# A Macaron block on one core: FFN 2 in two token groups, most of its rows routed during attention

## The chip, the core and the metric

The kernel is one program on one core of a Trainium2 chip. The metric is device time in microseconds (us), of three runs. The engines named here are TensorE (PE, with its weight loads as PEld), VectorE (DVE), ScalarE (ACT), GpSimd (POOL) and SyncE (SP), which issues most of the DMAs; SP's own rows of the profile are called SPq.

## The reference

The input is `x`, 4 batches of 512 tokens of 256 numbers, all in float32. With T = 2048 tokens, E = 16 experts, F = 128 and top-2 routing, the block is

```
x = x + 0.5 * ffn(layernorm(x))
x = x + attention(layernorm(x))          # 3 heads, each as wide as the model; mean of heads, fc, bias
x = x + 0.5 * ffn(layernorm(x))          # the same weights again

ffn(x): scores   = sigmoid(x @ gate_w)
        selected = top_2(scores + expert_bias);  w = their scores / (their sum + 1e-20)
        shared   = silu(x @ sg) * (x @ su) @ sd
        routed   = sum over the 2 selected e of  w_e * (silu(x @ G_e) * (x @ U_e) @ D_e)
attention(x): per head  Q, K, V = x Wq', x Wk', x Wv';  softmax(Q K' / 16) V
              then the mean over the heads, @ fc_w' + fc_b
```

## The kernel before, in words

**Exact products.** Each float32 operand is split into a high and a low part, and a product is three matmuls (`three_pass`: hi·hi, hi·lo, lo·hi). So every operand goes through two copies: ACT writes the high part from PSUM, DVE subtracts it and writes the low part. Transposes are matmuls with an identity.

**Stages.** (1) Norm and routing of all 16 token tiles (a tile is 128 tokens). (2) FFN 1. (3) Attention: 48 units (batch, head, block of 128 keys), 12 to a batch. (4) Norm and routing for FFN 2. (5) FFN 2. (6) Gather of the expert outputs, sum, shared expert, store.

**An FFN** works on sorted rows. Each of the 4096 (token, expert) pairs gets a slot; an expert's slots start at a multiple of 128. So `SLOT_TILES = 4096/128 + 15 = 47` tiles hold them in every case, each with the weights of one expert. `ffn(r, between)` walks steps `s`, the same loop on each engine: in step `s`, tile `s` is transposed (PE), split into `xt_ring` (ACT, DVE), tile `s-1` goes through gate and up (6 matmuls), its silu and product are formed, tile `s-3`'s hidden is transposed and split, tile `s-4` goes through down (3 matmuls), is copied to `y_buf` by ACT and stored to `y_dram` by SP. That is 47 + 4 steps. `between(s)` runs at the end of a step on each engine. PE reads the weight offsets of four tiles at a time from SBUF into registers (`pick_weights`). POOL gathers each tile's rows from `xn_dram` with an indirect DMA (`load`), up to 4 ahead.

**Routing** for r = 1 stands in the gap between attention and FFN 2: `front_turn`, `front_hi`, `front_lo` turn and split the normed rows of all batches, `front_router` gives the logits of batch 3, `choose` picks the two experts (tiles 0 to 11 during attention, 12 to 15 in the gap), `rank_tokens` counts tokens of each expert by matmuls with a triangle of ones, `slots` turns that into slots, `pick_tiles`, `pick_lanes`, `scale_tokens` and `index_tokens` invert the slots into a gather list, `experts` gives the weight offsets, `routing_weights` the two weights. Matmuls without use (`stay_busy`) stand between.

**Order.** Every engine runs its own program in the order written. In attention the extra work is cut into pieces by generators that all engines advance in step: `side_pieces(u, ...)` takes one piece in the middle of a unit (on POOL before the unit's `e_sp` subtraction, on DVE between the row maximum and the reciprocal), `side_pieces_late` takes one at the unit's end (batches 1 and 2: every unit; batch 3: from the unit `PER_BATCH // 2` on). `previous_front(b)` holds the norm, the float32 router and the routing of batch b-1. PE mixes the values of unit w about two units after its scores; `mix` of the last two units stands behind the loop.

**End.** `gather_pair(1, t)` on POOL reads the two expert outputs of each token from `y_dram` (32 indirect DMAs, 16 semaphores, a wait for landing at each eighth); `combine` on DVE adds them times their weights; the shared expert runs on PE, ACT and DVE (`shared_gu`, `shared_silu`, `shared_mul`, `shared_hi`, `shared_lo`, `shared_y`, `shared_sink`); SP stores each tile. All of it waits for the last tile of FFN 2.

## Time and profile before

| | |
|---|---|
| median of 3 runs | 578.79 us (578.08 to 579.34) |
| the profiled execution | 576.65 us |
| its span, first to last instruction | 575.4 us |
| mean granted TensorE clock | 0.939 of full |
| busy: PE, PEld | 465.3 us (81%), 408.9 us (71%) |
| busy: DVE, ACT, POOL | 337.1 (59%), 272.6 (47%), 253.8 us (44%) |
| chain that ended last | PE 57%, DVE 16%, issue 9%, ACT 6%, DMA 5%, POOL 5% |

A row of a timeline gives start, duration, engine, line, operation, output<-inputs and count, and in brackets how long the engine had been idle and what released it. PE rows overlap by about 0.15 us, since matmuls are pipelined; the distance between starts is the better measure. Line 324 is the helper of every three-pass product, so its rows are told apart by their operands.

### The profile page before, as it was taken

Reading aid. Unit: us, or ns where it says so; the run is one execution under the profiler, and the core shown is the slowest. Engines: PE = TensorE matmul, PEld = TensorE weight load, DVE = VectorE, ACT = ScalarE, POOL = GpSimd, SP = SyncE. Lnnn points to the kernel's source line nnn. Section 1 sums busy time; section 2 is a strip of 40 time slices with the busy share of each in tenths; the row PEclk is TensorE's granted clock in tenths of the full one; section 3 lists DMA queues with packets and bytes.
Section 4 is the critical chain, followed back from the end, with each engine's and each line's share of the span. In section 5 each row is a group of like instructions: output and inputs, shape, how many; then the busy total and the mean of one; then the engine's idle time right before and its main releaser. Section 6 shows DMA issues by size and latency. Waiting matters only on the chain.

```text
span 575.4 us, 9851 instructions
## 1 busy us (share of the span) xinstructions
PE 465.3 (81%) x3029; PEld 408.9 (71%) x3029; DVE 337.1 (59%) x925; ACT 272.6 (47%) x740; POOL 253.8 (44%) x259
## 2 busy tenths in 40 slices
PE   1675599999867997999899988999786799997432
PEld 0344488888655996898789977999755789886321
DVE  5478665555284666377538763635766566663554
ACT  4758266666424444345344544447333666662010
POOL 5356765553152542363237321422204555534655
PEclk9977799999989999999899999999897999999776
DMA  8642356466321100020001100003011455562444
GB/s 302 238 129 92 110 183 179 149 202 147 105 61 59 47 1 0 21 65 27 1 19 56 38 2 1 9 29 111 1 36 49 136 167 161 168 140 92 128 132 133
DMA packets 37808, 53.61 MB, mean 93 GB/s; under 512 B 5568, under 2 KB 30528, under 8 KB 37760
## 3 DMA queue, kind: packets, MB, share of 16 engines
q1 hardware_dynamic: 29760, 32.25, 16.8%
q0 software_dynamic: 7584, 20.72, 14.0%
q8 instruction: 27, 0.44, 0.3%
q14 instruction: 21, 0.17, 0.1%
q10 hardware_dynamic: 416, 0.02, 0.0%
HBM read 34.37 MB, written 18.61 MB: 92 GB/s over the span
## 4 chain that ended last, share of the span: by engine, by line
PE 57%; DVE 16%; issue 9%; ACT 6%; DMA 5%; POOL 5%; another core or an unknown queue 0%; SPq 0%; ACTq 0%; POOLq 0%; DVEq 0%
PE bank L324 47%; POOL late_pair L1545 4%; PE bank L330 3%; PE bank L543 2%; DMA late_pair<-y_dram,slot_i 2%; DMA raw<-xn_dram,gather_at 2%; PE bank L489 2%; DVE x_sb L1297 1%; DVE softmax_row L1418 1%; DMA x_sb<-in_x 1%; DVE e_sp L1307 1%; PE bank L376 1%; DVE v_sp L1428 1%; ACT v_sp L991 1%; DVE pick_lane L1180 1%
## 5 line engine op out<-in xcount | busy, mean ns | idle before, releaser
L1580 POOL DMA_INDIRECT raw<-xn_dram,gather_at x94 | 90.4, 962 | 87.3 <-PE bank L330 37.2
L1621 POOL TENSOR_TENSOR e_sp<-raw,e_sp 128x512 fp32r<-128x512 f32 x48 | 62.7, 1307 | 127.8 <-ACT e_sp L988 127.6
L324 PEld LDWEIGHTS bank<-v_sp,e_sp 128*128 128x128 f32 x576 | 75.5, 193 | 3.2 <-POOL e_sp L1621 0.3
L324 PE MATMUL bank<-v_sp,e_sp 128*128 128x256 f32 x576 | 77.7, 285 | 0.0
L324 PE MATMUL bank<-g_sp,xT 128*128 128x512 f32 x288 | 75.7, 398 | 1.4 <-DVE g_sp L1323 1.4
L979 ACT ACTIVATE raw<-bank,softmax_row 128x512 f32<-128x512 f32 x48 | 33.2, 692 | 58.0 <-DVE softmax_row L1418 57.9
L324 PEld LDWEIGHTS bank<-g_sp,xT 128*128 128x128 f32 x288 | 52.1, 190 | 11.0 <-DVE g_sp L1323 1.8
L1418 DVE TENSOR_REDUCE softmax_row<-bank 128x1 f32<-128x512 f32 x48 | 32.9, 686 | 38.0 <-PE bank L324 37.7
L324 PE MATMUL bank<-w_hi,e_sp 128*128 x188 | 50.5, 292 | 0.6 <-DVE e_sp L1307 0.6
L1307 DVE TENSOR_TENSOR e_sp<-bank,e_sp 128x128 fp32r<-128x128 f32 x94 | 27.4, 291 | 39.3 <-ACT e_sp L862 33.2
L324 PE MATMUL bank<-w_hi,v_sp 128*128 128x256 f32 x64 | 20.4, 397 | 35.5 <-DVE v_sp L1084 30.0
L324 PE MATMUL bank<-b_sp,xT 128*128 128x256 f32 x288 | 43.9, 288 | 3.7 <-DVE v_sp L1428 3.5
L324 PE MATMUL bank<-w_hi,xT 128*128 x188 | 45.4, 304 | 1.6 <-DVE xT L1311 1.6
L324 PE MATMUL bank<-w_hi,xt_late 128*128 x188 | 45.4, 304 | 1.4 <-DVE xt_late L1311 1.2
L1428 DVE SCALAR_TENSOR_TENSOR v_sp<-bank,softmax_row,v_sp 128x256 fp32r<-128x256 f32 x48 | 23.2, 484 | 34.9 <-ACT v_sp L991 34.3
L1545 POOL DMA_INDIRECT late_pair<-y_dram,slot_i x32 | 30.3, 948 | 29.6 <-DMA y_dram<-stage 13.3
L330 PE MATMUL bank<-ident,raw 128*128 128x128 f32 x212 | 41.2, 276 | 2.7 <-DMA raw<-xn_dram,gather_at 2.5
L885 ACT COPY stage<-bank 128x256 f32<-128x256 f32 x94 | 35.6, 378 | 15.9 <-PE bank L324 11.2
L324 PEld LDWEIGHTS bank<-w_hi,v_sp 128*128 128x128 f32 x64 | 16.0, 289 | 38.0 <-DVE v_sp L1084 31.9
L878 ACT ACTIVATE raw<-bank 128x128 f32<-128x128 f32 x94 | 26.7, 284 | 34.1 <-PE bank L324 29.1
L324 PEld LDWEIGHTS bank<-b_sp,xT 128*128 128x128 f32 x288 | 38.1, 190 | 6.2 <-DVE v_sp L1428 5.3
L1537 POOL DMA_INDIRECT stage<-y_dram,slot_i x32 | 31.4, 980 | 22.7 <-DMA y_dram<-stage 14.9
(204 smaller groups left out, 1086.7 us busy)
## 6 DMA issues: line engine op xcount, KB each, us to landing
y_dram<-stage SPq DMA_DIRECT2D x94, 128.0 KB
xn_dram<-xn_all SPq DMA_DIRECT2D x5, 512.0 KB, 4.3
stage<-in_w_pack SPq DMA_DIRECT2D x6, 384.0 KB, 5.4
raw<-in_w_pack SPq DMA_DIRECT2D x6, 384.0 KB, 3.1
x_sb<-in_x SPq DMA_DIRECT2D x4, 512.0 KB, 7.7
out<-x_sb SPq DMA_DIRECT2D x16, 128.0 KB
stage_more<-in_w_pack SPq DMA_DIRECT2D x5, 384.0 KB, 3.4
xn_dram<-raw SPq DMA_DIRECT2D x12, 128.0 KB, 1.7
```

The lines of the kernel that those rows point to most:

```text
L324: m = pe.matmul(dst, lhs[k][l], rhs[k][r], start=(first and k == 0 and i == 0), stop=(last and k == n - 1 and i == 2), skip_group_check=True)
L330: m = pe.transpose(dst[:, k * P:(k + 1) * P], src[:, k * P:(k + 1) * P], ident[:])
L878: act.activation(h_buf[:, g % 2, :], bank[GU_BANKS[g % 2]][:, 0:F], ACT.Silu).then_inc(s_silu, 1)
L885: act.copy(y_buf[:, d % Y_BUFS, :], bank[Y_BANKS[d % 2]][:, 0:H]).then_inc(s_y_copy, 1)
L979: act.activation(e32[:, i, :], bank[S_BANKS[i]][:], ACT.Exp, bias=row_max[:, i, :], accum_out=row_sum[:, i, :]).then_inc(s_exp, 1)
L1307: dve.tensor_tensor(ht_rows[:, v % 2, 1], bank[HT_BANK][:, 0:P], ht_rows[:, v % 2, 0].bitcast(F32), ALU.subtract).then_inc(s_hT_lo, 1)
L1418: dve.tensor_reduce(row_max[:, i, :], bank[S_BANKS[i]][:], AX, ALU.max, negate=True).then_inc(s_max, 1)
L1428: dve.scalar_tensor_tensor(out=v_sp[:, i, 1, :], in0=bank[V_BANK][:, 0:H], scalar=row_inv[:, i, :], in1=v_sp[:, i, 0, :].bitcast(F32), op0 ...
L1537: pool.indirect_dma_start(pair_buf[:, n % PAIRS, :], None, y_dram, at).then_inc(s_pair[n % PAIRS], 16)
L1545: pool.indirect_dma_start(late_pair[:, n, :], None, y_dram, at).then_inc(s_late[n % LATE_SEMS], 16)
L1580: pool.indirect_dma_start(row_buf[:, n % ROWS, :], None, xn_dram, bass.IndirectOffsetOnAxis(ap=gather_at[:, n:n + 1], axis=0)).then_inc(s_ ...
L1621: pool.tensor_tensor(e_sp[:, i, 1, :], e32[:, i, :], e_sp[:, i, 0, :].bitcast(F32), ALU.subtract).then_inc(s_e_lo, 1)
```

## The change

FFN 2's tokens are cut into two groups: batches 0 to 2 (`LATE_T = 12` tiles) and batch 3. Each group has its own tiles: `12*2 + 15 = 39` and `4*2 + 15 = 23`, together 62.

The sorted rows are no longer gathered by a list. `slab_dram` holds for each expert a slab of rows for each group. A token's place is its expert's base plus its rank so far, and POOL scatters the normed row to both its places (`slab_row`, 2 indirect DMAs a tile) out of `xn_late`, which DVE writes a second time (`row_again`). This is done batch by batch in new pieces of `previous_front`: `choose` for four tiles (now from an exponential on ACT, +1, reciprocal), `rank_again` (5 small matmuls), `slab_rows`, and for batch 3's turn `tile_table`, `pack_table`, `write_table`, `pair_slots`, `routing_weights` of the first group. SP clears the 128 rows behind each expert's last one (`clear_rest`, 16 DMAs of 128 KB from `zero_rows`), once for each group, and reads each tile with a plain DMA at an offset it loads from the table four at a time (`load_row`).

The gap between attention and FFN 2 is gone: FFN 2 begins after the last mix but one. The last mix, the norm and routing of batch 3, the second clear and the turning of all rows for the shared expert are pieces of `late_front` between steps 1 and 36 of FFN 2; `reload_batch` stands at steps 3, 5 and 7. `pick_tiles`, `pick_lanes`, `scale_tokens`, `index_tokens`, `stay_busy` are not called for r = 1. Gathers of the first group's pairs begin while FFN 2 still runs (pair n after tile 44 + n), and DVE sums one a step from step 48 (`early_combine`, 18 pairs); 8 places and semaphores instead of 32 and 16.

```diff
+    LATE_T = (B - 1) * TB
+    LATE_TILES = (LATE_T * TOPK + E - 1, TB * TOPK + E - 1)
+    SPLIT_TILE = LATE_TILES[0]
+    PAIRS_FROM = 44
+    COMBINE_FROM = 48
+    EARLY_COMBINED = 9
@@ side_pieces_late
-            if b == B - 1 and u % PER_BATCH >= PER_BATCH // 2:
+            if b == B - 1 and u % PER_BATCH >= PER_BATCH // 3:
@@ PE, previous_front
                 yield from prev_front(b - 1)
+                yield
+                rank_again(b - 1)
+                yield
+                yield
                 if b == B - 1:
-                    yield from choose(b * TB)
+                    yield
+                    pack_table(False)
...
@@ PE, pieces of FFN 2's steps
+            def late_front():
+                yield
+                mix(U - 1)
...
+                front_turn(1, FRONT_PAIRS - 2)
...
+                front_turn(1, FRONT_PAIRS - 1)
...
+                front_router(1, B - 1)
+                yield
+                turn_scores(1, B - 1)
...
+                rank_again(B - 1)
...
+                pack_table(True)
...
+                for n in range(FRONT_PAIRS - BATCH_PAIRS):
+                    yield
+                    yield
+                    front_turn(1, n)
+                    yield
@@ PE, behind attention
-            for w in MIXED_LATER:
-                if w == U - 1:
-                    front_turn(1, 0)
-                    front_turn(1, 1)
+            for w in MIXED_LATER[:-1]:
                 mix(w)
...
-            ffn(1, lambda s: None)
+            late_side = late_front()
+            ffn(1, lambda s: next(late_side, None))
@@ ACT
+                front_sigmoid(1, B - 1)
+                act.wait_ge(s_inv_sum, U)
+                act.wait_ge(s_warm, 2)
+                act.activation(row_sum[:, 0], minus_half[:, 0:1], ACT.Silu).then_inc(s_warm, 1)
@@ DVE, previous_front
+                for t in range((b - 1) * TB - 2, (b - 1) * TB):
+                    if t >= 0:
+                        row_again(t)
+                    yield
                 measure(b - 1)
                 yield
                 yield from prev_front(b - 1)
+                run(choose(1, (b - 1) * TB, b * TB))
+                yield
+                slab_rows(b - 1)
+                row_again((b - 1) * TB)
+                yield
+                row_again((b - 1) * TB + 1)
+                yield
                 if b == B - 1:
-                    yield from choose(1, 0, SPLIT_AT)
+                    row_again(b * TB - 2)
+                    tile_table(False)
+                    yield
+                    row_again(b * TB - 1)
+                    yield
+                    write_table(False)
+                    yield
+                    pair_slots(False)
+                    yield
+                    routing_weights(1, 0, LATE_T)
+                    yield
@@ DVE
+            def row_again(t):
...
+                dve.wait_ge(s_slab[t % 2], 16 * TOPK * (t // 2))
+                norm_rows(xn_late[t % 2], t).then_inc(s_again, 1)
@@ POOL
+            def slab_row(t):
+                if t % TB == 0:
+                    pool.wait_ge(s_addr, t // TB + 1)
+                if t < LATE_T:
+                    pool.wait_ge(s_again, t + 1)
+                src, done = (xn_late[t % 2], s_slab[t % 2]) if t < LATE_T else (xn_all[:, t, :], s_slab_late)
+                for k in range(TOPK):
+                    pool.indirect_dma_start(slab_dram, bass.IndirectOffsetOnAxis(
+                        ap=addr_i[:, k, t:t + 1].bitcast(U32), axis=0), src, None).then_inc(done, 16)
@@ POOL, gather_pair
-                        if n and n % BURST == 0:
...
+                        if PAIRS_FROM + n < TILES[1]:
+                            pool.wait_ge(s_xt, BASE[1] + PAIRS_FROM + n)
@@ POOL, previous_front(3), behind the last slab_row
+                    pool.wait_ge(s_comb, NT * TOPK)
+                    pool.memset(zero_rows, 0.0).then_inc(s_zeros, 1)
@@ SP
+            def load_row(n, rows):
...
+                if i == 0:
+                    sp.wait_ge(s_zero, 16 * E * (1 + late))
+                    sp.wait_ge(s_experts, 2 + late)
+                if i % PER_LOAD == 0:
...
+                if n >= ROWS:
+                    sp.wait_ge(s_xt, BASE[1] + n - ROWS + 1)
+                sp.dma_start(row_buf[1][:, n % ROWS, :], slab_dram[bass.ds(rows["at"][i % PER_LOAD], P), :])
+            def clear_rest(late):
+                sp.wait_ge(s_zero_at, 1 + late)
+                sp.wait_ge(s_zeros, 1)
+                for e in range(E):
+                    sp.dma_start(slab_dram[bass.ds(at[e % PER_LOAD], P), :], zero_rows).then_inc(s_zero, 16)
+            def late_front(s):
+                if s in (3, 5, 7):
+                    reload_batch((s - 3) // 2)
+                if s == 16:
+                    clear_rest(True)
```

## Rows read from the trace of the kernel before

**Rows 1.** Windows: length; PE, PEld, DVE, ACT, POOL busy (count); clock; DMA share; GB/s

```profile
235.00:293.00 58.00, 55.02 (x350) 49.64 (x349) 37.64 (x88) 26.68 (x62) 25.53 (x22) 0.97 0.09 28
351.00:406.60 55.60, 55.60 (x374) 51.22 (x373) 27.07 (x98) 30.29 (x65) 16.77 (x14) 1.00 0.12 39
406.60:440.70 34.10, 25.06 (x150) 19.18 (x148) 25.10 (x70) 12.55 (x30) 4.26 (x5) 0.80 0.06 20
440.70:522.20 81.50, 73.05 (x565) 67.15 (x564) 45.35 (x141) 51.26 (x188) 42.40 (x45) 1.00 0.54 149
522.20:575.40 53.20, 22.24 (x96) 18.53 (x96) 25.23 (x48) 4.41 (x8) 30.34 (x32) 0.76 0.40 122
```

**Rows 2.** Timeline of PE in the gap: two front turns, the router

```profile
406.61 1.04 PE L376 MATMUL bank<-ident,xn_all 128*128 128x128 f32 x8
...
421.16 1.57 PE L324 MATMUL bank<-xT,gate_sp 128*16 128x512 f32 x6 [0.70 <-DVE xT L1072]
```

**Rows 3.** Timeline of PE in FFN 1: a fold (L489), then the next tile

```profile
85.87 1.89 PE L489 MATMUL bank<-route 128*128 128x256 f32 x8
...
87.71 0.38 PE L330 MATMUL bank<-ident,raw 128*128 128x128 f32 x2
```

**Rows 4.** Timeline of DVE in the gap: statistics, the start and end of one choice, a scan

```profile
410.93 1.40 DVE L1031 BATCH_NORM_STATS2 stats<-x_sb 128x6 f32<-128x256 f32 x4
...
424.09 0.23 DVE L1114 TENSOR_TENSOR route<-bank,bias_sb 128x64 f32<-128x64 f32 x1 [2.98 <-PE bank L398]
...
425.90 0.23 DVE L1140 TENSOR_TENSOR choice<-route 128x64 f16<-128x64 f32 x1
...
426.74 0.20 DVE L1151 TENSOR_TENSOR_SCAN ends<-unround,rounded 128x17 f32<-128x17 f32 x1
```

**Rows 5.** Timeline of ACT: one table load

```profile
420.40 1.28 ACT L789 ACT_TABLE_LOAD   x1
```

**Rows 6.** Timelines of POOL, DVE, then PE, in the last units of batch 1

```profile
284.92 1.33 POOL L1621 TENSOR_TENSOR e_sp<-raw,e_sp 128x512 fp32r<-128x512 f32 x1 [4.90 <-ACT e_sp L988]
...
285.13 1.39 DVE L1297 TENSOR_TENSOR x_sb<-x_sb,route 128x256 f32<-128x256 f32 x1
...
287.60 0.68 DVE L1418 TENSOR_REDUCE softmax_row<-bank 128x1 f32<-128x512 f32 x1
289.39 0.42 DVE L1287 TENSOR_TENSOR xT<-bank,xT 128x256 fp32r<-128x256 f32 x1 [1.11 <-ACT xT L846]
...
289.87 3.02 PE L324 MATMUL bank<-xT,a_sp 128*128 128x512 f32 x12 [1.16 <-DVE xT L1287]
```

**Rows 7.** Timelines of POOL, then PE, in the first units of batch 2 of attention

```profile
302.95 0.96 POOL L1537 DMA_INDIRECT stage<-y_dram,slot_i  x1
304.22 0.95 POOL L1537 DMA_INDIRECT stage<-y_dram,slot_i  x1 [0.30 <-issue]
...
308.89 1.31 POOL L1621 TENSOR_TENSOR e_sp<-raw,e_sp 128x512 fp32r<-128x512 f32 x1
...
313.12 1.60 PE L324 MATMUL bank<-v_sp,e_sp 128*128 128x256 f32 x12
```

**Rows 8.** DMA issues (KB each, median us to landing), then the instructions of L1703

```profile
xn_all<-xn_dram SPq DMA_DIRECT2D x3, 512.0 KB, 4.9
...
L1703 SPq DMA_DIRECT2D y_dram<-stage x94: 319/320/628, 73.3 to 522.0; - x94
```

**Rows 9.** Instructions of L1545 (ns min/median/max); timelines of the end

```profile
L1545 POOL DMA_INDIRECT late_pair<-y_dram,slot_i x32: 945/949/951, 524.6 to 570.3; - x32
...
528.97 0.68 DVE L1084 TENSOR_TENSOR v_sp<-bank,v_sp 128x512 fp32r<-128x512 f32 x1
529.71 0.38 PE L324 MATMUL bank<-w_hi,v_sp 128*128 128x256 f32 x1 [1.71 <-DVE v_sp L1084]
...
533.99 1.28 DVE L1099 SCALAR_TENSOR_TENSOR x_sb<-bank,x_sb 128x512 f32<-128x512 f32 x2
...
573.12 0.48 DVE L1238 SCALAR_TENSOR_TENSOR x_sb<-late_pair,weight,x_sb 128x256 f32<-128x256 f32 x1 [0.35 <-DMA late_pair<-y_dram,slot_i]
```

More of the change, by code:

```diff
@@ L58, in macaron @@
     AT_LOADS = -(-SLOT_TILES // PER_LOAD)
+    IN_SLAB = "a place in a slab: the expert is at most E - 1 and a rank at most the tokens routed so far"
     BOUNDED = "tile_expert is a count of is_le over E ends, held at E - 1 by a min"
@@ L1626, in pool_program @@
             norm_scale(2, B - 1)
[L1627 to L1636 removed]
+            pool.wait_ge(s_row_norm, NT + TB)
+            for t in range(LATE_T, NT):
+                slab_row(t)
+            for t in range(NT):
+                gather_pair(1, t)
         def sp_program():
```

716 lines of the change are left out of this document (456 added, 260 removed).

## The prediction

> **What bounds the kernel now.** I read the windows first [rows 1]. They cut the end of the run into three: the gap between attention and FFN 2 (34.1 us, PE busy 25.1, much of it matmuls without use), FFN 2 (81.5 us, PE busy 73.1) and the end (53.2 us, PE 22.2, POOL 30.3). Attention stands before them, and in batch 3 PE is busy for all of 55.6 us. So PE bounds attention and FFN 2. The chain of waits then says what bounds the rest. In the gap it is a line of small steps from DVE to PE and back. At the end it is POOL's 32 gathers, one after the other, then a last sum at 573.12 and the store, 1.8 us [rows 9]. The change attacks both idle stretches and pays in FFN 2, where PE has no room.
>
> All sums are against the profiled execution: span 575.4 us, 576.65 us in all. The median of the runs is 578.79, 2.1 higher, and I add the difference to that.
>
> **The gap: what goes.** The front turns begin at 406.61, when the last mix but one is done [rows 2]; the first tile of FFN 2 was turned at 440.7. If nothing in attention moved, FFN 2 would start 34.1 us earlier.
>
> **Attention: what comes.** I placed the new pieces by counting yields.
>
> - Batches 1 and 2: `choose` is piece 9, late in unit 9; `slab_rows` with `rank_again` is piece 10. DVE is on the path there: it starts the row maximum of unit 10 at 287.60, straight behind unit 9's last piece, and the next batch's PE work waits for DVE until 289.87 [rows 6]. A choice over four tiles takes 2.05 us from 424.09 to 426.13 [rows 4], and +1 and the reciprocal add two small operations of 0.2 us. 2.5 us and the rank sums (under the router's 1.57 us [rows 2], I take 0.5) go in whole: 3.2 us a batch, 6.4 for two.
> - Batch 2, POOL: pieces 0 and 1 bring 4 scatters beside the gathers of units 0 to 3. An indirect DMA takes about 1.26 us from start to start, so two slab rows put 5.0 us into a stretch in which POOL was full. The `e_sp` part for unit 2 was ready at 310.2 and needed at 313.12 [rows 7]: 2.5 us of it shows with what DVE adds.
> - Batch 3: `slab_rows` is piece 10 (unit 7), `tile_table` 12 and `pack_table` 13 (both unit 8). `row_again(10)` shares its buffer with row 8, so DVE waits for that scatter to land (2.5 us of issue, then about 1.7, as a gather's 2.7 from its start), and the table, 11 chained small operations at 0.2 to 0.25 us, comes behind it. PE reaches `pack_table` some 5 us before the table: 5.4 us with the rank sums.
> - Behind that, SP. The zero rows are set on POOL after the fourth slab row, and only then do 16 clears of 128 KB go out. A store of 128 KB holds SP's queue for 0.32 us [rows 8], with four reads of offsets about 7 us for all; landing about 1.7. Then the first row load lands 2 us later. On my clock PE is ready about 4.5 us before the row.
>
> Sum: 6.4 + 2.5 + 5.4 + 4.5 = 18.8 us. Bounds: 8, if DVE's pieces hide in the mixes and the scatters run beside PE; 24, if DVE's waits for landing add up in every batch.
>
> A rule bears on the first item. Beside POOL's `e_sp` subtraction of 1.33 us one DVE sum took 1.39 us, where a subtraction of the same width took 0.42 a little later [rows 6]. The Trainium skill ("SBUF — State Buffer", Who interferes with whom) says that a DVE instruction with two SBUF inputs and a GpSimd instruction that reads SBUF exclude each other for a whole instruction. The row agrees. `choose` has such operations; by the rule up to 1.3 us a batch would come on top, 3.9 in all, where I add nothing, since `choose` stands at the unit's end and POOL may be through. The rule changes the sum by that much at most.
>
> **FFN 2: 15 more tiles.** 51 steps took 81.5 us, 1.60 each [rows 1]. 66 steps: 24.0 us more. Nothing hides this; the tiles are walked whether rows are in them or not. Bounds: 21.5 (PE's busy 73.05 us over 51 steps, 1.43 each) and 25 (some of the waits of a start come again with the second group).
>
> **FFN 2: PE's pieces.** The fold of FFN 1 shows what an insertion costs: it starts at 85.87 and the next tile's turn at 87.71, so its 1.84 us are added whole [rows 3]. Inserted are the last mix (1.45 us by the pitch of such rows, [rows 7]), 8 front turns of 4 transposes (eight transposes take 1.04 [rows 2]: 4.2 us), the router (1.4 [rows 2]), score turns, rank sums and table (1.05 together). 8.1 us.
>
> **FFN 2: what DVE, ACT and SP put in PE's way.** DVE is busy 45.4 of 81.5 us, 0.89 a step, ACT 51.3, 1.0 a step [rows 1]. But a tile's two parts must be ready within a step, so I give a DVE piece 0.5 us of cover a step and count the rest. Statistics for four tiles 1.75 (1.40 plus five small ones), the sum of attention's output 1.3, a choice 2.0, slab rows 1.2, the table 2.3, slots 1.2, weights 1.4 [rows 4] (small ones at 0.2): beyond cover 7.5 us, less 1 that falls into waits that PE has anyway. ACT loads a table three times (silu, sigmoid, silu), 1.28 us each [rows 5], before FFN 2's first silu and beside the router: 2.5 beyond PE's own piece. SP's second clear again takes 7 us, at step 16; row 20 is queued behind it and is due four steps later, 6.4 to 8 us: 2 us. Three reloads of 512 KB, 4.9 us to landing together [rows 8]: 0.5. PE comes out of a wait at the start, and in the gap and at the end, where it waits, its granted clock is 0.80 and 0.76 against 1.00 in FFN 2 [rows 1]: 1.2. Sum 12.7. Bounds: 4 (pieces ride in PE's insertions) and 22 (no cover, and both clears hold rows up).
>
> The early sums are free in this account: 0.48 us a step from step 48 [rows 9], inside the 0.5. If that cover is gone, 18 times 0.2 us.
>
> On the queue, too, the skill has a rule ("DMA: Bandwidth & Descriptors", Queues, rings and completion order): each DMA engine takes a ring's descriptors in order. By it every row load issued behind the clears waits for all their 2 MB. Each clear's cost above stands on SP's issue time instead; the rule would bring nothing more as long as the issue is the slower of the two.
>
> **The end.** Before, 53.2 us [rows 1]. After, 24 of 32 gathers are issued when the last tile is done; 8 remain, from 2.3 us behind it (last gather begins at about 13, its data are there at 16). So the shared expert ends last. Gate and up take 2.7 us a batch (12 matmuls of 512 columns at the router's pitch [rows 2]), down 1.45. Down of batch 0 started at 529.71, 7.5 us after the stage began, behind a sum [rows 9]; I put it at 6.4. From there: 1.5, then twice 2.7 + 1.5, then y of batch 3 waits for two sinks and a sum on DVE (1.28 [rows 9], 1.0, 0.68): it runs from 19.7 to 21.1. Sink, last sums and store: 24.7, and 0.3 for clock. 25 us, so 28.2 less. Bounds: 22 less (PE at its half clock through most of it, or DVE late), 30 less.
>
> **Sum:** -34.1 + 18.8 + 24.0 + 8.1 + 12.7 - 28.2 = +1.3. 578.79 + 1.3 = **580.1 us**, at the edge of what a measurement of this kernel can tell from no change (about 0.2%, 1.2 us). With the low bounds: -34.1 + 8 + 21.5 + 8.1 + 4 - 30 = -22.5; with the high ones: -34.1 + 24 + 25 + 8.1 + 22 - 22 = +23.
>
> **Rivals.**
>
> 1. *The pieces hide* (faster). Attention's three places cost what DVE cannot hide, 11 us in place of 18.8, the clear is through before PE is ready, and in FFN 2 PE's insertions give DVE and ACT the time for theirs: 5 in place of 12.7. For it: DVE is busy only 37.6 of 58 us in batch 1 and 45.4 of 81.5 in FFN 2 [rows 1]. Against it: the rows in which PE waits for DVE with all that idle time around [rows 6]. -34.1 + 11 + 24 + 8.1 + 5 - 28.2 = -14.2: 564.6 us.
> 2. *The row loads are late* (slower). SP gets rows 4 ahead, but the load of row s+4 stands behind the store of tile s-4, which is copied at the end of a step. That leaves about 4 us for an issue and a landing of some 2.4, and every fourth time four offsets must be read first. If this wait shows at each of the 16 reads with 0.8 us, PE stands 13 us longer: 592.9 us. For it: stores and loads now share one queue, where before POOL gathered beside it. It decides from the point where issue, read and landing exceed three steps, 4.8 us.
> 3. *The end is not 25.* The shared expert's chain crosses DVE, ACT and PE four times, and when PE waits its clock falls (0.76 in this window [rows 1]). With matmuls at half clock, 12 us of PE work become up to 18 and the end 30 to 31: 585.5 us.
> 4. That the overlap isn't had at all (FFN 2 starts late because a row, the zeros or the table are missing) is within the bound of 24 for attention: 585.1.
>
> **How the numbers follow.** Forecast 0.42, with its own range 574 to 586 (attention ±4 and FFN 2's waits ±4, taken together); of this 0.12 is faster, 0.10 the same, 0.20 slower. Rival 1: 0.33. Rival 2: 0.13. Rivals 3 and 4: 0.12. Faster 0.45, the same 0.10, slower 0.45. Range 565 to 593: it reaches rival 1's and rival 2's time and leaves half of each outside, 0.2 with the tails.
>
> **What would show it.** In the profile after: FFN 2's first turn of a tile at about 425 us (below 417: rival 1; above 431: more than I counted); PE idle at the table's pack in batch 3, released by DVE; the first row turn released by a DMA; in FFN 2, 66 steps in about 126 us with DVE as releaser around steps 12 to 19, and not a row load at each fourth tile (that is rival 2); a last stretch of 25 us with POOL done some 9 us before the end. If FFN 2 takes under 116 us or attention's batches keep 58 us each, the account is wrong on the side of rival 1.

## Result, and the profile after

| | median | range | runs |
|---|---|---|---|
| before | 579.07 us | 578.08 to 580.92 | 4 |
| after | 604.24 us | 602.90 to 606.33 | 4 |

The ratio of the times is 1.0434, with a 95% interval of 1.0394 to 1.0474: slower by 25 us, where 580.1 (565 to 593) was forecast. The profiled execution has a span of 605.0 us, 29.6 more than before.

The windows of the kernel after come first, with the columns of [rows 1]. The stretches are: batch 1 as in [rows 1]; batch 2, from the G product of its start to that of batch 3; batch 3 with what follows up to FFN 2's first turn; FFN 2; the end.

```profile
235.00:293.00 58.00, 52.27 (x339) 47.56 (x337) 39.91 (x105) 26.55 (x62) 24.23 (x21) 0.95 0.09 28
293.25:364.83 71.58, 61.91 (x366) 54.91 (x364) 42.99 (x115) 27.05 (x64) 33.51 (x31) 0.88 0.12 38
364.83:441.00 76.17, 65.20 (x398) 58.22 (x395) 41.16 (x125) 28.43 (x64) 34.88 (x32) 0.90 0.20 67
441.00:577.40 136.40, 111.57 (x808) 102.83 (x808) 79.96 (x275) 78.76 (x262) 31.70 (x33) 0.90 0.57 174
577.40:605.00 27.60, 19.66 (x96) 15.84 (x96) 16.37 (x30) 4.41 (x8) 8.17 (x8) 0.93 0.41 125
```

The books close like this. The first turn of FFN 2 is at 441.0, and the front turns of before were at 406.6 [rows 2]: attention has grown by 34.4 us, and the whole gap of 34.1 is eaten. FFN 2 takes 136.4 in place of 81.5 [rows 1], 54.9 more. The end takes 27.6 in place of 53.2. -34.1 + 34.4 + 54.9 - 25.6 = 29.6. Against the forecast of +1.3, attention took 15.6 us more than its term, FFN 2 10.1 and the end 2.6.

Attention, from the same G product at 228.9 (before) and 229.0 (after), grows in three steps: 3.2 us up to the G of batch 2, then 13.2 (71.58 against 58.4, 289.87 [rows 6] to 348.29), then 14.7 up to the last mix, then 3.15 for the first row. The first three steps are 31.1 us over three batches. These are the sums over the same three stretches, G to G and then to the last mix, of the kernel before and of the kernel after:

```profile
sum 177.74, PE 171.43 PEld 155.28 DVE 103.37 ACT 84.55 POOL 69.11; mean PE 57.14 PEld 51.76 DVE 34.46 ACT 28.18 POOL 23.04
sum 208.81, PE 185.53 PEld 165.68 DVE 124.58 ACT 82.65 POOL 94.06; mean PE 61.84 PEld 55.23 DVE 41.53 ACT 27.55 POOL 31.35
```

So PE stood still for 17.0 us more and was busy for 14.1 us more, with 27 matmuls more in 1098: most of the busy part is a lower granted clock, 0.93, 0.88 and 0.90 in the three batches, where it was 0.95, 1.00 and 1.00. PE's waits of the kernel after from 230 to 441 us (sum, times, longest) name the places:

```profile
PE bank L504 <- issue: 7.9, 2, 4.0
PE bank L524 <- DVE tile_of L1294: 5.0, 1, 5.0
PE bank L357 <- POOL e_sp L1876: 3.9, 1, 3.9
PE bank L387 <- issue: 3.5, 4, 1.4
PE bank L357 <- DVE v_sp L1684: 1.7, 1, 1.7
PE bank L387 <- ACT route L841: 1.1, 1, 1.1
```

L504 is the first matmul of `rank_again`, at the ends of batches 1 and 2. Read DVE's rows there, of the same kernel, and then PE's:

```profile
290.59 0.23 DVE L1250 TENSOR_TENSOR choice<-route 128x64 f16<-128x64 f32 x1
290.73 0.68 DVE L1674 TENSOR_REDUCE softmax_row<-bank 128x1 f32<-128x512 f32 x1
292.52 0.43 DVE L1469 TENSOR_TENSOR xT<-bank,xT 128x256 fp32r<-128x256 f32 x1 [1.11 <-ACT xT L931]
...
293.05 0.21 PE L504 MATMUL bank<-choice,before 128*128 128x64 f16 x1 [3.96 <-issue]
293.25 5.08 PE L357 MATMUL bank<-xT,a_sp 128*128 128x512 f32 x12
```

The choice is there at 290.8, and yet PE starts at 293.05. It waits for the bank that the rank sums share with the turn of the next batch's rows. That bank is free when DVE has copied it (L1469). This copy waits for ACT, which waits for the row maximum (L1674), which stood behind the choice. Then comes the part that I had not counted: G's twelve matmuls run largely at half clock, 5.08 us where they took 3.02 [rows 6]. The distance to the G of the next head is 19.4 us, before 17.0. Behind the G of batch 3 it is 19.2.

### The profile page after: what moved, and what is told of

It is laid out like the page before. It is cut to its first block and busy times, and to the rows that moved or that the text cites. A ratio compares the mean times of both kernels' runs of the same rounds, so it can differ in the third digit from the quotient of the medians.

```text
span 605.0 us, 10777 instructions
## 1 busy us (share of the span) xinstructions
PE 490.7 (81%) x3143; PEld 433.7 (72%) x3143; DVE 359.4 (59%) x1044; ACT 286.0 (47%) x785; POOL 242.2 (40%) x245
## 5 line engine op out<-in xcount | busy, mean ns | idle before, releaser
L357 PE MATMUL bank<-v_sp,e_sp 128*128 128x256 f32 x576 | 83.4, 298 | 3.9 <-POOL e_sp L1876 3.9
L357 PEld LDWEIGHTS bank<-v_sp,e_sp 128*128 128x128 f32 x576 | 80.7, 206 | 7.9 <-POOL e_sp L1876 5.0
L357 PE MATMUL bank<-w_hi,xt_late 128*128 x248 | 63.4, 317 | 3.3 <-DVE xt_late L1493 1.8
L1791 POOL DMA_INDIRECT late_pair<-y_dram,slot_i x32 | 31.1, 971 | 77.6 <-PE bank L363 57.7
L357 PEld LDWEIGHTS bank<-g_sp,xT 128*128 128x128 f32 x288 | 53.2, 194 | 11.5 <-DVE g_sp L1505 1.8
L357 PE MATMUL bank<-w_hi,e_sp 128*128 x218 | 60.7, 300 | 0.4 <-DVE e_sp L1489 0.3
L1829 POOL DMA_INDIRECT raw<-xn_dram,gather_at x47 | 46.3, 985 | 33.9 <-PE bank L363 21.5
L1674 DVE TENSOR_REDUCE softmax_row<-bank 128x1 f32<-128x512 f32 x48 | 33.0, 687 | 39.6 <-PE bank L357 39.3
L964 ACT ACTIVATE raw<-bank 128x128 f32<-128x128 f32 x109 | 30.7, 282 | 46.2 <-PE bank L357 30.9
L1498 DVE TENSOR_TENSOR raw<-raw,bank 128x128 f32<-128x128 f32 x109 | 31.1, 285 | 31.5 <-ACT raw L964 19.1
L357 PEld LDWEIGHTS bank<-w_hi,xt_late 128*128 128x128 f32 x248 | 45.5, 202 | 5.7 <-issue 4.6
L608 PE MATMUL bank<-ident,raw 128*128 128x128 f32 x109 | 31.3, 287 | 20.3 <-DVE e_sp L1489 17.5
L357 PEld LDWEIGHTS bank<-w_hi,e_sp 128*128 128x128 f32 x218 | 42.7, 196 | 2.7 <-issue 1.1
L357 PE MATMUL bank<-xT,a_sp 128*128 128x512 f32 x144 | 41.3, 443 | 2.9 <-DVE xT L1447 1.7
```

Of the source, the lines that this page charges most:

```text
L357: m = pe.matmul(dst, lhs[k][l], rhs[k][r], start=(first and k == 0 and i == 0), stop=(last and k == n - 1 and i == 2), skip_group_check=True)
L608: pe.transpose(bank[HT_BANK][:, 0:P], h_buf[:, v % 2, :], ident[:]).then_inc(s_hT, 1)
L964: act.activation(h_buf[:, g % 2, :], bank[GU_BANKS[g % 2]][:, 0:F], ACT.Silu).then_inc(s_silu, 1)
L1498: dve.tensor_tensor(h_buf[:, g % 2, :], h_buf[:, g % 2, :], bank[GU_BANKS[g % 2]][:, F:GU], ALU.mult).then_inc(s_act, 1)
L1674: dve.tensor_reduce(row_max[:, i, :], bank[S_BANKS[i]][:], AX, ALU.max, negate=True).then_inc(s_max, 1)
L1791: pool.indirect_dma_start(late_pair[:, n % LATE_PLACES, :], None, y_dram[0:(SPLIT_TILE if t < LATE_T else TILES[1]) * P, :], at).then_inc( ...
```

## Experiments

The runs came in five sets, each on another chip. In two of them (e1 to e4, e13 to e16) the kernel before took 576.5 and 579.4 us, as in the first measurement (the first sort); in the other three (e5 to e8, e9 to e12, e17 with e18) 565 us (the second sort). What goes with a set may thus be the chip's. Kernels are compared by their ratio to the kernel before in their own set; 0.01 is 5.7 us. The kernel after again, in a set of the second sort, gave nearly its ratio:

**e9_after_again.** No edit.

> The kernel after, unchanged, as the measure for the runs beside it: the ratio to the kernel before again 1.043, within its interval. Its profile also tells whether two things belong to the kernel or to the one chip they were seen on: ACT's stall of 4.7 us while eight scatters are issued, and the waits around the early gathers (27.4 us for the 14 steps from 46). In two runs of other kernels that shared this code neither showed. If they are the chip's, steps 17 to 21 take about 15 us in place of 20.2.

1.0413 (1.037 to 1.0456). Both things belong to the set and not to the kernel: ACT does not stand, and the last 19 steps take 30.0 us, where they took 38.4. Steps 17 to 21 take 16.1 us in place of 20.2. Attention has grown by 30.7 us here, from the first G to FFN 2's first turn, if the kernel before runs in this set as in its first profile. Windows of this kernel, FFN 2 and end:

```profile
434.10:557.70 123.60, 106.16 (x804) 99.01 (x804) 79.91 (x274) 78.73 (x261) 29.23 (x31) 0.93 0.62 187
557.70:585.00 27.30, 18.63 (x99) 15.06 (x99) 17.11 (x32) 4.88 (x10) 10.33 (x11) 1.00 0.50 152
```

The boundary of these rows lies 1.3 us ahead of the first gate matmul (558.99), at which the windows of the kernel before and after are cut. Counted as those are, FFN 2 takes 124.9 us in place of 136.4, and the end 26.0 at full clock in place of 27.6. The other runs are counted in this way below.

**e13_before_profile.** The kernel before again, to compare windows.

> The kernel before, unchanged, for a profile of it on the chip of the later runs (565 us there, 579 on the first). Theory: what makes this chip quicker lies ahead of attention and in the granted clock, the stretch from the G of batch 1 to PE ready for FFN 2 is 177 to 178 us as on the first, FFN 2 80 to 82 and the end 51 to 54. Rival: FFN 2 itself is shorter there by 5 us or more; then the growth of FFN 2 (42 us with the kernel after, 54.9 on the first chip) has to be told anew.

This was one execution, in a set of the first sort (579.5 us), so the question about the second sort stays open. It repeats the first profile in attention, 58.4 us from the G of batch 2 to that of batch 3. FFN 2 takes 83.3 us from 442.0 on (81.5 in the first profile), and the end 53.0. The profiles of before can thus be trusted to about 2 us a stretch.

### Attention

**e14_own_rows.** 

```diff
+        again = raw[:, 1024:1536].rearrange("p (i h) -> p i h", i=2)
@@ row_again, slab_row
-                norm_rows(xn_late[t % 2], t).then_inc(s_again, 1)
+                norm_rows(again[:, t % 2], t).then_inc(s_again, 1)
@@ DVE and POOL, previous_front(2)
+                for q, _ in enumerate(prev_front(b - 1)):
+                    if b == 2 and 2 <= q < 5:
+                        row_again(q - 1)    # POOL: slab_row(q - 1)
...
```

> Only the second norms' own buffer, and batch 0's rows 1 to 3 scattered in units 5 to 7 of batch 2 in place of units 0 and 1, where POOL gathers; all else as after. Theory (the pile of scatters and gathers costs batch 2 some 6 us beside the wait for the choice): PE's 3.9 us for POOL's part of e_sp goes with the half clock behind it, batch 2 from G to G falls from 70 to 71.6 us to 65 to 66, ratio 1.033. Rival (POOL is late by other work): under 1 us.

1.0335 (1.0296 to 1.0374), 5.7 us less than after by the ratios. Batch 2 falls from 71.58 to 64.05 us (e15, in the same set and without this edit, has 71.02), and no PE wait for POOL is left in it. The rows are of the kernel after, then of e14:

```profile
322.99 1.23 PE L357 MATMUL bank<-v_sp,e_sp 128*128 128x256 f32 x4 [3.89 <-POOL e_sp L1876]
```

```profile
295.58:359.63 64.05, 58.34 (x367) 52.49 (x364) 43.15 (x115) 27.09 (x64) 33.42 (x31) 0.93 0.13 42
```

So the pile cost 7.0 to 7.5 us, where I had put 2.5.

**e7_warm.** 

```diff
+            def warm(n):
+                for _ in range(n):
+                    pe.matmul(bank[SIDE_BANK][:], w_hi[:, 0:P], w_hi[:, 0:BANK], ...)
@@ rank_again(b < B - 1) and pack_table(False), behind wait_bank7()
+                    warm(14)    # and warm(20)
```

> PE runs 14 matmuls without use ahead of the rank sums of batches 1 and 2 and 20 ahead of the tile table, while it waits for DVE there. Theory (each of these waits is paid twice, once as itself and once as half clock behind it): G behind the rank sums takes 3.1 us in place of 5.1, twice, and the scores behind the table 2 in place of 2.9: 4 to 6 us less, 597 to 599. Rival (what comes behind waits for DVE anyway, or the matmuls delay the rank sums as much): 0 to 1 us, 602 or more.

Slower: 1.0563 (1.0511 to 1.0615), against 1.0413 and 1.0434 for the kernel after: on the rival's side, and worse than no gain. The matmuls stand behind the wait for the bank, and that is the wait that counts, as the releaser now shows:

```profile
285.66 1.65 PE L497 MATMUL bank<-w_hi 128*128 128x512 f32 x3 [3.91 <-DVE xT L1477]
```

They start only when the bank is free, run at a granted clock of 0.70 themselves and cost 4.8 us (285.66 to the G at 290.47). Behind them the distance from G to G is 17.2 us, where e9 has 18.5 and the kernel after 19.4, and in batch 3 17.1, where both have 19.2. The second price is thus real, 1.3 to 2.2 us a place, but it can't be bought back with work that waits for the same thing: the half of the theory about the clock is right, the gain is not there.

**e1_table_first.** 

```diff
-                    row_again(b * TB - 2)
                     tile_table(False)
+                    row_again(b * TB - 2)
```

> In batch 3 the tile table is worked out ahead of the tenth row's second norm, which waits for a scatter to land, and no longer behind it. Theory (the waits at the seam stand in a row, each hiding the next): PE's 5.0 us for the table falls under 1.5, but PE then meets the first row load, which still hangs on the zero rows and 16 clears, some 5 us earlier: the first turn of FFN 2 moves from 441.0 by 1.5 us at most, and the time from 604.2 to 602.5 to 604. Rival (waits of attention add up, each with its half clock): 5.0 plus 2 us of clock go in whole, first turn at 434 to 435, 597 to 598.

1.0471 (1.0414 to 1.0528), no gain. The first turn is at 440.86, released by the first row after 3.59. But the wait for the table falls only from 5.01 to 3.91 us, where the theory wanted it under 1.5, so this run doesn't tell what the whole wait is worth. Batch 3 takes 73.0 us to the last mix, as in the kernel after: the 1.1 us came back in other waits. Why so little went, these rows show: the table's rounding in the kernel after, then the same operation in e1 with POOL's row beside it.

```profile
417.82 0.37 DVE L1285 TENSOR_SCALAR rounded<-rounded 128x16 f32<-128x16 f32 x1
```

```profile
414.75 1.85 DVE L1285 TENSOR_SCALAR rounded<-rounded 128x16 f32<-128x16 f32 x1
415.29 1.27 POOL L1876 TENSOR_TENSOR e_sp<-raw,e_sp 128x512 fp32r<-128x512 f32 x1
```

In the kernel after, DVE first waits 2.16 us for the scatter to land. In e1 that wait is gone from in front of the table, but the rounding takes 1.5 us longer and ends at 416.60, POOL's subtraction at 416.56. In e15 it takes 1.95 us and again ends 0.04 us behind the subtraction.

**e2_zeros_early.** 

```diff
@@ POOL: the memset of zero_rows from piece 13 to piece 2 of batch 3
@@ slab_rows
+                if b == B - 2:
+                    dve.tensor_copy(zero_at[0:1, :], slab_to[0:1, :]).then_inc(s_zero_at, 1)
...
```

> The zero rows are set early in batch 3, and the ends of the slabs are handed to SP right behind the ranks of batch 2, so the first 16 clears are through some 10 us earlier. The table stays late. Theory (the clears set the first row): the 3.15 us that PE stands at the first row go, first turn at about 437.5, time 600 to 601. Rival (reading the offsets and the row's own landing set it, the clears only stand beside them): under 1 us, 603.5 or more.

1.0367 (1.033 to 1.0404), 3.9 us less than after. The first turn is at 434.97, and not released by a DMA. The theory is right on the row; the time fell by 0.8 us more than the row's 3.15.

**e15_zeros_table.** Both edits.

> Zero rows and slab ends early, and the tile table ahead of the tenth row's second norm, both on the kernel after (each alone is measured). Theory (at the seam they stand in a row: with the table alone nothing was won, with the zeros alone 4 us): together 6 to 9 us less than after, first turn at 426 to 429 with G of batch 1 at 225.7, ratio 1.028. Rival (the wait for DVE's table was worth nothing, PE then meets the next wait): 4 us, as with the zeros alone, ratio 1.034.

1.0341 (1.0301 to 1.0381), 1.5 us under the zeros alone, within the intervals; the number is the rival's. The first turn is 207.4 us behind the G of batch 1, with the zeros alone 206.2. But PE's wait at the table is 3.96 us here. Only 1.0 of the 5.0 was taken away, as in e1, so neither run shows what the wait is worth.

**e8_spread.** The edits of e14 for all of batch 0's rows, and:

```diff
@@ choose(1, ...), behind the maxima
+                if r == 1 and t1 < NT:
+                    yield
@@ DVE, previous_front (PE's rank_again and pack_table one piece later)
-                run(choose(1, (b - 1) * TB, b * TB))
-                yield
-                slab_rows(b - 1)
-                row_again((b - 1) * TB)
+                for _ in range(3):
+                    next(chosen)
+                yield
+                run(chosen)
+                yield
+                slab_rows(b - 1)
+                yield
...
```

> Attention's pieces in other places: the choice of a batch is cut in two pieces, each behind another row maximum; rank sums and slab rows one piece later; second norms in a buffer of their own, batch 0's rows scattered in units 5 to 8 of batch 2 (past its gathers) and batch 2's behind the tile table. Theory (attention's 34 us are placement: 2 times 5.3 at the ends of batches 1 and 2, 6.7 where the scatters pile up beside gathers, 7 at the table): attention's shift falls by 12 to 18 us, and the first turn to 425 to 430, unless clears and zeros hold the first row, which are not moved: then 434 to 437. Time 594 to 600. Rival (the pieces cost the same wherever they stand, as DVE is what they load): first turn at 439 or later, 602 or more.

1.0427 (1.0385 to 1.047): no gain that can be told, and by the time the rival; the profile tells why. Batch 1 takes 61.1 us from G to G, as before the change, batch 2 61.6. Batch 3 still takes 74, though no wait for the table is left in it. PE is ready for FFN 2 at 420.65, and then stands for the first row, since zeros and clears were not moved:

```profile
432.05 1.31 PE L364 MATMUL bank<-ident,stage 128*128 128x128 f32 x4 [11.40 <-DMA stage<-slab_dram]
```

### FFN 2

**e3_clear2_pool.** POOL issues the second 16 clears, behind its scatters.

```diff
-                if s == 16:
-                    clear_rest(True)
@@ POOL, behind the slab rows of batch 3
+                pool.dma_start(slab_dram[bass.ds(at[e % PER_LOAD], P), :], zero_rows).then_inc(s_zero2, 16)
```

> The second 16 clears are issued by POOL behind its scatters, not by SP between row loads. Theory (the clears' place in SP's queue costs twice: the rows queued behind, and the stall of ACT and DVE at step 18): both the 3.7 us for a row and the 5.2 us for ACT's and DVE's part go, with the half clock behind them, 10 to 13 us, 592 to 594. Rival A (the stall belongs to the DMA traffic or to POOL's scatters): only the row wait and 1 us of clock go, 599 to 600. Rival B (POOL's own issue of a clear is slow, 1 us and more, and its gathers come late): 604 and more, with the last gather later than 1493 thousandths of the way, that is past 595 us.

1.0400 (1.0371 to 1.0429), 2 us less than after, within the intervals: nearest to rival A, since a step of 8.6 us stays at the same place, now without the clears, while the next two fall from 10.0 to 4.9 us. (The odd figure in rival B's sentence has no meaning; its bound is 595 us.) ACT's row, of the kernel after and of e3:

```profile
485.46 0.28 ACT L964 ACTIVATE raw<-bank 128x128 f32<-128x128 f32 x1 [4.67 <-remote]
```

```profile
482.57 0.28 ACT L964 ACTIVATE raw<-bank 128x128 f32<-128x128 f32 x1 [4.61 <-remote]
```

In both it ends as the eighth scatter in a row goes out (issued at 484.29 and 482.22).

**e5_spaced.** 

```diff
@@ slab_row
+                    if t >= LATE_T:
+                        pool.wait_ge(s_xt, BASE[1] + 16 + 2 * ((t - LATE_T) * TOPK + k))
```

> POOL issues the eight scatters of batch 3 two steps of FFN 2 apart in place of back to back; SP's second clear stays where it is. Theory A (a row of back to back indirect DMAs holds ACT up: in the kernel after, ACT stood 4.7 us at L964 until the last of eight scatters was out): the step of 8.3 us at 17 to 18 falls under 4, with the half clock behind it, time about 596 to 598 against 602 to 604 unchanged. Theory B (the stall hangs on the place in ACT's own instruction stream or on SP's clears, since it came at the same step in four kernels): the step stays at 8 us.

1.0357 (1.029 to 1.0424) against 1.0413 for after, unclear. One long step stays, 9.5 us with a wait of 7.4 in it, but it is the one up to row 20 and has another cause: row 20 is queued behind the clears. This set was of the sort in which ACT doesn't stand in any kernel, so the run says nothing on ACT. It shows the wait for the row bare, as e9 does; the rows are e9's:

```profile
472.00 9.88 SPq L1970 DMA_DIRECT2D slab_dram<-stage  x16
482.47 0.35 SPq L1959 DMA_DIRECT2D stage<-slab_dram  x1
484.52 0.69 PE L363 MATMUL bank<-ident,stage 128*128 128x128 f32 x2 [7.66 <-DMA stage<-slab_dram]
```

**e10_clear2_spaced.** 

```diff
-                if s == 16:
-                    clear_rest(True)
+                if 18 <= s < 18 + E:
+                    next(late_clear)    # one of the 16
```

> SP issues the second 16 clears one a step, from step 18 on, between a store and the next row load, in place of all 16 at once at step 16. Theory (a row load stands behind 16 clears, and PE waits 7.4 to 8.1 us for it): the long step goes, with half clock behind it; 9 to 11 us less than after, ratio to before 1.025. Rival (the 2 MB of clears delay the rows by their traffic, at whatever rate they are issued): 2 to 4 us less, and short waits for rows in each step from 18 to 33.

1.0328 (1.0284 to 1.0371) against 1.0413 beside it: 4.8 us, between the two. The long step is gone, and steps 17 to 21 take 7.1 us in place of 16.1, which is the theory's 9. But the rest of FFN 2 takes 2.2 more (the later rows show short waits, 0.8 us in all), so that it falls from 124.9 to 118.1. The place in SP's queue was what counted, and the rival's traffic may have a small part.

**e6_no_early.** 

```diff
@@ gather_pair(1, 0)
+                    pool.wait_ge(s_xt, DONE[1])
@@ DVE
-                next(combining, None)    # in the steps
+            run(combining)    # behind ffn(1, between2)
```

> The early gathers and the early sums of FFN 2 are taken out of its steps and stand behind its last tile; the rest is as after. One look, read by windows. Theory A (gathers beside the tiles cost pace): the last 19 steps, 27.4 us from step 46 to 60 in the kernel after, go at 1.45 a step, 20 to 21, and the wait of 4.6 us at step 47 is gone, so FFN 2 ends 8 to 10 us earlier. Rival (they are free, as I counted): under 2 us. The end stretch grows by about 30 us in both.

This was one execution, 607.4 us. In this set the rival is nearer: FFN 2 takes 122.2 us against 124.9 in e9 and 125.2 in e5, and the end 45.2 against 26.0. The early gathers and sums cost 2.7 to 3.0 us in FFN 2 and save 19 at the end. For the sets of the first sort, where the last steps were slower, this run says nothing.

**e4_tiles_50.** 

```diff
-    LATE_TILES = (LATE_T * TOPK + E - 1, TB * TOPK + E - 1)
+    LATE_TILES = (32, 18)
-    PAIRS_FROM = 44
-    COMBINE_FROM = 48
+    PAIRS_FROM = 32
+    COMBINE_FROM = 36
```

The tokens of this input fit 50 tiles; every routing fits only 62.

> FFN 2 walks 32 and 18 tiles in place of 39 and 23; the early gathers and sums begin 12 steps earlier. Theory (a tile costs the pace of a step, whatever is in it): 12 tiles at 1.56 to 1.60 us, 18.7 to 19.2 us less, 585 to 586. Rival (with the pieces of batch 3 still taking their 40 steps, DVE and ACT set the pace of part of FFN 2): the steps that stay grow, 13 to 15 us less, 589 to 591.

1.0296 (1.0262 to 1.0329): 8 us less, under both theory and rival. Why, e12 and e17 show.

### All of it

**e11_all.** e8, with zeros and slab ends early, e10's clears, and batch 3's scatters one a step.

> All of it: the choice in two pieces, rank sums one later, second norms in their own buffer and batch 0's scatters past the gathers, zero rows and slab ends early, the table ahead of batch 2's scatters, the second clears and batch 3's scatters one a step. From the kernel in which attention's pieces were moved: its first turn at 432.1 held a wait of 11.4 us for the first row, and its long step in FFN 2 one of 7.8. Theory (waits of placement, and nothing comes in their place): both go, first turn at 421 to 423, 25 to 28 us less than after, ratio to before 0.995 to 1.0. Rival (the row's landing and the table take over at the seam, at some 5 us): ratio 1.01.

1.0109 (1.0051 to 1.0168), and **e18_all_again**, the same kernel:

> The kernel with all changes of place again, with 62 tiles, as the measure for the run beside it. It had 1.011 of the time before; again between 1.005 and 1.017. If this is the chip on which ACT stood at the scatters and the early gathers: the scatters, one a step, bring no step above 2.5 us, the first gathers still one of 4.

1.0172 (1.0108 to 1.0237). Of the 23 us that the kernel after costs in these sets (e9), 17 are back by e11 and 14 by e18. It is the rival's number. The windows of e11: batch 1, batch 2, batch 3 to PE ready, FFN 2, end (counted from the first gate matmul at 537.25, FFN 2 takes 115.7 and the end 26.0).

```profile
223.10:283.10 60.00, 55.15 (x357) 49.75 (x357) 39.24 (x96) 26.96 (x64) 25.49 (x22) 1.00 0.09 27
283.10:346.30 63.20, 58.41 (x362) 52.37 (x362) 43.82 (x115) 27.15 (x63) 33.31 (x30) 0.95 0.13 43
346.30:420.60 74.30, 63.25 (x398) 55.48 (x398) 42.21 (x135) 26.76 (x60) 33.87 (x31) 0.98 0.19 65
421.00:535.90 114.90, 103.67 (x805) 95.50 (x805) 80.23 (x277) 80.56 (x265) 30.27 (x32) 0.99 0.67 202
535.90:563.20 27.30, 18.59 (x99) 15.03 (x99) 17.12 (x32) 4.84 (x10) 10.55 (x11) 1.00 0.50 154
```

At the seam one row wait of 1.17 us is left. What stays of attention's growth is 5 us in batch 2 and, above all, batch 3: 74.3 us against 58.3 before, in which PE was busy throughout. In e11 PE is busy for 63.3 us of it, 5 more. The rest are its waits there, 10.7 us in eight short places (sum, times, longest):

```profile
PE bank L358 <- POOL e_sp L1889: 4.7, 3, 2.3
PE bank L358 <- DVE v_sp L1693: 2.6, 3, 1.3
PE bank L505 <- DVE choice L1252: 2.2, 1, 2.2
PE bank L388 <- ACT route L843: 1.2, 1, 1.2
```

The pieces were moved and batch 3 did not get shorter: here e8's rival, that the pieces cost the same wherever they stand, fits. No run takes pieces out of batch 3, so that it is DVE's and POOL's load that sets its length is argued and not shown.

**e16_all_thin.** The choice and the table of batch 3 each cut in two steps of FFN 2 (a `yield` more in each, what follows one or two steps later).

> The kernel with all changes of place, and in FFN 2 also batch 3's choice and tile table each cut in two steps, the pieces behind them one or two steps later. Theory (a DVE piece above its cover of half a step's time stands in PE's way): the steps of 2.5 and 2.9 us shrink to 1.8 to 2.0, 2 to 3 us less than 569.6, ratio 1.006. Rival (PE's own pieces there and the ACT tables set these steps): within 1 us.

1.0126 (1.0073 to 1.0178): nothing, the rival. The two steps shrink to about 2 us, others grow by as much: steps 13 to 19 take 13.6 us together, as in e11. This set was of the first sort, and with the scatters one a step no step from 17 to 22 exceeds 2.2 us, where e14 and e15 in the same set have one of 8.6 and 8.8; one of 4.3 is left where the early gathers begin, and the last 19 steps still take 38.7 us.

**e12_all_50.** e11 with e4's edit, the clears two a step.

> As the kernel with all of it, but 32 and 18 tiles in place of 39 and 23 (second clears two a step, early gathers and sums 12 steps earlier). Theory (a tile costs 1.5 to 1.6 us where nothing else is in the way): 18 to 19 us less than the kernel with all of it, ratio to before 0.965. Rival (the early gathers meet the split and cost what they did in the first run with 50 tiles, 10 us): 8 to 10 us less.

0.9974 (0.9926 to 1.0022): 8 us under e11 by the ratios, the rival's number, and 3 by the medians. The profile has the reason why the tiles brought so little:

```profile
509.05 1.00 POOL L1800 DMA_INDIRECT late_pair<-y_dram,slot_i  x1 [29.76 <-PE bank L364]
512.50 0.48 DVE L1421 SCALAR_TENSOR_TENSOR x_sb<-late_pair,weight,x_sb 128x256 f32<-128x256 f32 x1 [3.71 <-DMA late_pair<-y_dram,slot_i]
513.33 0.30 PE L609 MATMUL bank<-ident,raw 128*128 128x128 f32 x1 [3.77 <-DVE e_sp L1490]
```

DVE has reached the first early sum, its gather has only just been issued, and the next tile's part is queued behind the sum. e4 has the same row, so its missing microseconds are in part these:

```profile
527.96 0.48 DVE L1420 SCALAR_TENSOR_TENSOR x_sb<-late_pair,weight,x_sb 128x256 f32<-128x256 f32 x1 [3.54 <-DMA late_pair<-y_dram,slot_i]
```

**e17_50_late_sums.** 

```diff
-    COMBINE_FROM = 36
+    COMBINE_FROM = 40
@@ behind ffn(1, between2)
+            run(combining)
```

> As the kernel with all changes of place and 50 tiles, but its early sums begin at step 40 in place of 36 (those left over follow the last tile). In the run with sums from step 36, DVE stood 3.7 us at the first sum for a gather that could start only at 509.05, behind the store of tile 31, with the next tile's part queued behind it. Theory (this wait and its clock are why 12 tiles brought 3 us in place of 18): the steps of 5.6, 1.9 and 2.5 us there fall to 1.5 or 2 each, and the kernel is 12 to 17 us under the one with all and 62 tiles, ratio to before 0.98 to 0.99. Rival (the 12 tiles are not worth more than 3 to 5 us, whatever the sums do): ratio 1.00 or more.

0.9852 (0.9793 to 0.9911), 18 us under e18's ratio, 15 by the medians (557.4 and 572.5): the theory. FFN 2 takes 102.8 us, in e18 117.1. A tile costs 1.2 to 1.5 us by these three numbers, and this is the one version that beats the kernel before; it does so by tiles that another input may need.

## Why the prediction was wrong

**The gap** (-34.1) and **the end** (-28.2 forecast, -25.6 measured) held. The shared expert ends last, as forecast. In the timeline of the kernel after, the last gather begins 12 us before the end, and PE starts batch 3's down after it has stood for DVE:

```profile
592.94 0.95 POOL L1791 DMA_INDIRECT late_pair<-y_dram,slot_i  x1 [0.30 <-issue]
599.64 0.39 PE L357 MATMUL bank<-w_hi,v_sp 128*128 128x256 f32 x1 [2.68 <-DVE v_sp L1191]
```

The end is 27.6 and not 25. Its first gate and up matmuls run at half clock, and down of batch 0 starts 7.9 us in, not 6.4. In e9 and e11, at full clock, it starts 6.2 us in, and the end takes 26.0. So 1.6 of the 2.6 us are clock, and 1.0 is what stands behind, where PE waits for DVE.

**Attention** (18.8 forecast, upper bound 24; 34.4 measured, 30.7 in e9) is the step that failed first. The list of places was right, but not what they cost: POOL's part was mis-sized, and the half clock behind each wait and batch 3's own growth had no term in this sum at all.

- *Ends of batches 1 and 2, 3.2 each.* Right in size: 3.2 at the G of batch 2, and by the path named there (row maximum behind the choice). Missing was the half clock behind each wait, 1.3 to 2.4 us each time; e7's distance of 17.2 from G to G shows it. I had seen it in the gap and at the end of before (0.80 and 0.76 [rows 1]) and used it only in FFN 2 and the end. The rule on POOL and DVE added nothing here: no operation of the choice took over 0.55 us. It bore on the table (e1), where I hadn't looked.
- *POOL in batch 2, 2.5.* Measured 7.0 to 7.5 (e14). I counted four scatters; `slab_row(1)`, piece 11 of batch 1, falls into unit 0 of batch 2 as well. Three slab rows stand beside the gathers.
- *Table in batch 3, 5.4.* The wait was there, 5.01 us for `tile_of`, with the landing of the scatter (2.16) and the chain of small operations (2.4) that I had named. What it was worth stays open: e1 and e15 take away only 1.1 and 1.0 us of it, and in e8 and e11, with other pieces moved too, it is gone and batch 3 is no shorter than in the kernel after. Beside it, batch 3 lost 9.7 us that I had not put anywhere: 6.9 more of PE's busy time (65.2 against 58.3, at a clock of 0.90) and 2.8 in short waits.
- *Zeros, clears, first row, 4.5.* Measured 3.15, and 3.9 by e2.

**FFN 2** (44.8 forecast; 54.9 measured, 43.4 in e9 if the 81.5 of before hold there) is the second step that failed. In one sort of set the sum stood near the truth, but by luck, with two errors that cancel. The *tiles* (24.0 for 15) cost 1.2 to 1.5 us each, so 18 to 23, about my lower bound of 21.5 or under it. The *second clear* (2.0) made PE wait 7.7 us where nothing else stood, and 9.0 with the clock behind it (e10). I let 16 clears take 7 us of SP's queue; they take 9.5 to 10.7 in the sets of the second sort and 13.8 to 14.1 in the others, and row 20 comes behind all of them. *ACT's tables*: 2.5 forecast; at the router two loads of 1.28 and what lies between hold ACT from 463.37 to 466.55, 3.2 us, and DVE's part of the tile waits 3.73. The *reloads* (0.5) cost nothing: PE waited for none. (The 4.9 us of [rows 8] is the median of one reload, not of three together.) In the set of the first measurement 11.5 us come on top of e9's: 4.1 from step 17 to 21, where ACT stands beside the scatters, and 8.4 in the last 19 steps, with the early gathers, less 1 elsewhere. No term of the sum stands for either. I had called the *early sums* free. They nearly are in e9 (2.7 us with the gathers, e6). They are not where the gather is late (e12).

**Rivals.** Rival 1 (564.6) was wrong at each of its three places. Rival 2 (a row late at each fourth tile) didn't happen: one row was late, by the clears. Rival 3 had the right mechanism, half clock after waits, in the wrong stretch. Rival 4's outcome came, by another cause: FFN 2 began at 441.0, when the gap of before would have ended, but the row was missing for 3.15 us only, and the other 31 are attention's own growth. The signs in the prediction pointed the right way: a first turn above 431 was to mean that attention cost more than counted.

**The rule on queues.** The Trainium skill ("DMA: Bandwidth & Descriptors", Queues, rings and completion order) says that each DMA engine takes a ring's descriptors in order; by it a row behind the clears waits for all their 2 MB. In e9 the row's load was itself issued only at 482.47, and PE had it 2.05 us later: the issue was the slower of the two, and no run here shows the rule at work.

## What to carry to other kernels

A wait that an engine off the critical path adds is paid in PE's time at the next shared thing: a bank, a buffer, or the queue that a small load stands in. Before a burst (scatters, clears) is placed, look at what is queued behind it on its engine, and issue it one a step; that alone took 9.0 us out of four steps and 4.8 out of the time (e10). And take a wait out of a copy of the kernel before counting it as a gain, and look whether it has really gone: one of 3.9 us for POOL was worth 5.7 of the time and 7 of its batch, one of 3.15 for a row 3.9, and of the longest (5.0 for the table) two edits took away only a fifth.

## What had not been expected of the hardware

- Each of PE's waits of 3.9 to 5.0 us in attention is followed by matmuls at half clock (G in 5.08 us in place of 3.02): the granted clock is 0.73 in the 18.8 us from 351 to 369.8 and 0.88 in batch 2, against 1.00 in e11's batch 1. In e7 matmuls placed behind the wait came too late to help.
- On the chips on which the kernel before took 576 to 580 us, ACT stood idle for 4.6 to 6.8 us while POOL issued eight indirect DMAs back to back (the kernel after, e1 to e4, e14, e15; "remote" as releaser in most), and steps with early gathers took 1.95 us. SP was slow in the same stretch: its second 16 clears took 13.8 to 14.1 us where SP issued them at once. On the chips with 565 us the same code showed no such stand, 9.5 to 10.7 us for the clears and 1.7 us a step (e5 to e9). With scatters and clears one a step the stand is gone on a chip of the first sort too (e16, against e14 and e15). It isn't the clears, since e3 has it without them. What holds ACT, and why only on these chips, wasn't found.
- 16 clears of 128 KB, each four with their offsets read ahead, take SP's queue 9.9 us in e9, 0.62 each. A store of the same size took 0.32 [rows 8]. That the reading of the offsets is the difference is likely but not shown.
- A DVE operation on 128x16 numbers took 1.85 and 1.95 us in place of 0.37 when it began ahead of POOL's subtraction, and ended 0.04 us behind it (e1, e15).
